# Leftover keys of an attention sweep taken in eight pieces in its middle, with constant products at the joints

## The reference

```python
scores = jnp.einsum('bhqd,bhkd->bhqk', qh, kh)       # 16 heads, 1024 queries, 6404 keys
attn = jax.nn.softmax(scores, axis=-1)
ctx = jnp.einsum('bhqk,bhkd->bhqd', attn, vh)
```

## Time and profile before

| | us |
|---|---|
| median of 3 runs | 3082.24 (3079.79 to 3084.54) |
| the profiled execution | 3080.51 |
| its span | 3078.7 |
| mean granted TensorE clock | 0.991 |

### The profile page before, as it was taken

How to read it: one execution, slowest core, us unless ns; L and a number is a source line. 1 busy time by engine, 2 the same in 40 slices (tenths; PEclk the granted TensorE clock), 3 DMA queues, 4 the chain that set the end, 5 groups by cost and what they waited for, 6 DMA issues and landing times.

```text
span 3078.7 us, 54520 instructions
## 1 busy us (share of the span) xinstructions
PE 3009.3 (98%) x18701; PEld 1140.2 (37%) x18701; DVE 467.2 (15%) x1308; ACT 2519.7 (82%) x2893; POOL 206.1 (7%) x732
## 2 busy tenths in 40 slices
PE   7999999999999899999999998999999999999999
PEld 5333333323334433333323334666522222332257
DVE  4200001001011400111101004544200000000012
ACT  3899999999933499999999995322499999999963
POOL 4000000000000000000000002000000000000000
PEclk9999999999999999999999999999999999999999
DMA  7122122112220112122211223110011111111110
GB/s 198 54 63 64 58 63 68 38 37 63 63 75 0 29 58 69 54 63 65 64 38 39 63 63 112 32 37 1 8 38 37 37 37 54 47 38 36 37 38 8
DMA packets 167028, 157.27 MB, mean 51 GB/s; under 512 B 20872, under 2 KB 121724, under 8 KB 166844
## 3 DMA queue, kind: packets, MB, share of 16 engines
q1 hardware_dynamic: 159872, 149.27, 16.1%
q0 software_dynamic: 1088, 3.34, 0.3%
q10 hardware_dynamic: 5884, 2.08, 0.3%
HBM read 121.89 MB, written 32.91 MB: 50 GB/s over the span
## 4 chain that ended last, share of the span: by engine, by line
PE 94%; DVE 3%; DMA 1%; issue 1%; ACT 1%; SPq 1%; ACTq 0%; DVEq 0%
PE PS L2343 40%; PE PS L2362 31%; PE PS L774 5%; PE PS L759 5%; PE PS L761 2%; PE PS L1114 2%; PE PS L1104 1%; PE PS L1572 1%; PE PS L1569 1%; PE PS L1148 0%; PE PS L1105 0%; PE PS L2323 0%; PE PS L2253 0%; PE PS L2329 0%; PE PS L1134 0%
## 5 line engine op out<-in xcount | busy, mean ns | idle before, releaser
L2110 ACT ACTIVATE probs<-PS 128x1024 f32<-128x1024 f32 x2496 | 2283.0, 1227 | 37.8 <-PE PS L2362 32.9
L2343 PE MATMUL PS<-probs,vr 128*32 128x512 f32 (+1 forms) x9984 | 1324.3, 603 | 1.9 <-DVE accs L2590 1.9
L2362 PE MATMUL PS<-qs,kr 35*128 35x512 f32 (+2 forms) x4992 | 1064.4, 481 | 8.7 <-ACT probs L2110 3.3
L2362 PEld LDWEIGHTS PS<-qs,kr 35*128 35x128 f32 x4992 | 448.0, 184 | 1181.9 <-ACT probs L2110 816.0
L797 ACT ACTIVATE probs<-PS 128x512 f32<-128x512 f32 x192 | 114.5, 598 | 273.6 <-PE PS L759 145.5
L1939 POOL COPY vr<-vs 128x72 f32 (+1 forms) x624 | 157.8, 253 | 2668.9 <-PE PS L2343 2466.5
L2343 PEld LDWEIGHTS PS<-probs,vr 128*32 128x32 f32 x9984 | 197.2, 108 | 339.2 <-issue 272.1
L774 PEld LDWEIGHTS PS<-wide,probs 128*128 128x128 f32 x1280 | 152.7, 195 | 17.5 <-issue 16.5
L774 PE MATMUL PS<-wide,probs 128*128 128x128 f32 x1280 | 155.1, 279 | 0.5 <-DVE kf L832 0.5
L2590 DVE COPY accs<-PS 128x512 f32<-128x512 f32 x12 | 8.3, 692 | 750.1 <-PE PS L2329 750.1
L759 PE MATMUL PS<-xT,wide 128*128 128x512 f32 x224 | 106.7, 594 | 1.0 <-DVE probs L816 1.0
(11 more groups left out here) (315 smaller groups left out, 1185.8 us busy)
## 6 DMA issues: line engine op xcount, KB each, us to landing
kr<-key_pieces SPq DMA_DIRECT2D x1248, 64.0 KB
key_pieces<-kparts SPq DMA_DIRECT2D x172, 96.0 KB, 2.8
kr<-mask_strips SPq DMA_DIRECT2D x624, 4.0 KB
values<-kf SPq DMA_DIRECT2D x34, 216.0 KB, 4.2
vs<-values SPq DMA_DIRECT2D x2, 3672.0 KB, 16.1
c_T<-turned_context SPq DMA_DIRECT2D x18, 192.0 KB, 4.0
key_pieces<-probs SPq DMA_DIRECT2D x32, 96.0 KB, 2.9
c_in<-turned_context SPq DMA_DIRECT2D x16, 192.0 KB, 4.3
```

The costliest lines, as they stand in the source:

```text
L2110: sc.activation(prob[n % RING][:, :, q0:], PS[:, bank:bank + 2, q0:], ACT.Exp, scale=SCALE).then_inc(p_ready, 1)
L2343: last = te.matmul(PS[32 * j:32 * j + 32, 7, q0:], vr[s.buf(c)][:, at_v:at_v + 32], prob[(n + j // 2) % RING][:, j % 2, q0:], start=fresh, ...
L2362: last = te.matmul(o, kr[b][own, p, :], qs[own, T8 // 2 * s.hh + p, 512 * s.qh + q0:512 * s.qh + 512], start=True, stop=True)
```

## The change

The leftover work leaves the sweep's end. The four score products are made one at a time in round 9 (LEFT_ROUND), behind quads (0,1), (1,0), (1,1) and (2,0) of that round; the exponential follows round 9 on ACT; the product of values is cut into four of 128 columns, behind the same quads of round 10. The first piece waits for what the whole did (left_in in a first sweep, bank 6 free). The item of round 9 moves to the last chunk of round 10, and that of round 10 to the first chunk of round 11. Where the rounds were one hardware loop, rounds 9 and 10 are written out between two loops. At each joint three constant products into bank 6 stand between scores(1, 0) and values(s, 0, 0), and eight into bank 5 ahead of the flag of the third attention. DVE's copy of bank 7 waits for the sweep's last values, and two other waits for pv_done make up for the order that the leftover product gave.

```diff
+LEFT_ROUND = EXP_ROUND - 1
@@ early_dve
                 dve.wait_ge(left_ready, 2)
+                dve.wait_ge(pv_done, SWEEPS[2].quads)
@@ SP, sweeps with w % 4 == 2
                                 sp.wait_ge(left_ready, s.w)
+                                sp.wait_ge(pv_done, s.quads)
@@ ACT
                             exps(c, p)
-                            if prev and (c, p) == (0, 1):
-                                exps_left(prev)
                     with act.Fori(1, EXP_ROUND) as i:
...
+                    exps_left(s)
...
-                    if s.w % NSW == NSW - 1:
-                        exps_left(s)
@@ PE, ahead of the flag of the third attention
+                idle_products(8, 5)
                 pe.wait_ge(flag_ready, a + 1)
@@ PE
-                def left_scores(s):
+                def left_free(s):
                     if s.w % NSW == 0:
                         pe.wait_ge(left_in, LEFT_IN * (a + 1))
                     if s.w:
                         pe.wait_ge(left_done, s.w)
...
+                    if s.w % NSW == 2:
+                        if a == 0:
+                            pe.wait_ge(early_ev, EARLY_AT[0] + 3)
+                        else:
+                            pe.wait_ge(r_cen, (0, 1, 3)[a])
+                    own = [(w, i) for w in range(s.w + 1) for i in range(1, ROUNDS_S) if w < s.w or i < LEFT_ROUND]
+                    pe.wait_ge(v_ev, NTILE + sum(len(later_items(w, i)) for w, i in own))
+                def left_score(s, tt):
+                    if tt == 0:
+                        left_free(s)
...
+                def left_value(s, k):
+                    if k == 0:
+                        pe.wait_ge(left_done, s.w + 1)
+                    last = te.matmul(PS[:, 7, k * P:k * P + P], v_left[:, s.hh, :], p_left[:, k * P:k * P + P], start=False, stop=True, skip_group_check=True)
...
+                def left_slot(s, i, c, g):
+                    slot = 2 * c + g - 1
+                    if i == LEFT_ROUND and 0 <= slot < 4:
+                        left_score(s, slot)
+                    if i == LEFT_ROUND + 1 and 0 <= slot < 4:
+                        left_value(s, slot)
...
                     if prev:
                         values(prev, prev.n - 1, 0)
-                        left_scores(prev)
                     scores(0, 1)
                     if prev:
                         values(prev, prev.n - 1, 1)
-                        left_values(prev)
...
+                            if prev and (c, g) == (1, 0):
+                                pe.wait_ge(v_ev, NTILE + sum(len(later_items(w, i)) for w in range(s.w) for i in range(1, ROUNDS_S)))
+                                idle_products(3, 6)
                             values(s, c - 1, g)
...
+                            if i == LEFT_ROUND:
+                                items = []
+                            if i == LEFT_ROUND + 1:
+                                items = [None] * (TC - 1) + later_items(s.w, LEFT_ROUND)
+                            if i == LEFT_ROUND + 2:
+                                items = later_items(s.w, i - 1) + items
...
                                     values(s, i * TC + c - 1, g)
+                                    left_slot(s, i, c, g)
...
-                        with pe.Fori(1, ROUNDS_S) as i:
+                        with pe.Fori(1, LEFT_ROUND) as i:
...
+                        for c in range(LEFT_ROUND * TC, (LEFT_ROUND + 2) * TC):
...
+                        with pe.Fori(LEFT_ROUND + 2, ROUNDS_S) as i:
...
                     if s.w % NSW == NSW - 1:
-                        left_scores(s)
                         for g in range(2):
                             values(s, s.n - 1, g)
-                        left_values(s)
@@ DVE
                     dve.wait_ge(left_used, s.w + 1)
+                    dve.wait_ge(pv_done, s.quads + 2 * s.n)
```

More of the change, by code:

```diff
@@ L2383, in _ @@
                                     values(s, i * TC + c - 1, g)
-                                if c < len(items):
+                                    left_slot(s, i, c, g)
+                                if c < len(items) and items[c]:
                                     later_pe(pe, *items[c])
@@ L2388, in _ @@
                     else:
-                        with pe.Fori(1, ROUNDS_S) as i:
+                        with pe.Fori(1, LEFT_ROUND) as i:
+                            for c in range(TC):
+                                for g in range(2):
+                                    scores(c, g, i)
+                                    values(s, c - 1, g, i)
+                        for c in range(LEFT_ROUND * TC, (LEFT_ROUND + 2) * TC):
+                            for g in range(2):
+                                scores(c, g)
+                                values(s, c - 1, g)
+                                left_slot(s, c // TC, c % TC, g)
+                        with pe.Fori(LEFT_ROUND + 2, ROUNDS_S) as i:
                             for c in range(TC):
```

15 lines of the change are left out of this document (7 added, 8 removed).

## The result

The changed kernel takes 3141.03 us (median; 3133.99 to 3153.87), the one before beside it on the same chip 3081.01 us (3078.21 to 3084.54). The ratio is 1.0192, interval 1.0168 to 1.0216: 60 us slower, where 22 us slower had been forecast and the range ended 33 us above the kernel before. The profiled execution after took 3144.03 us, its span is 3142.3 us, 63.6 us more than before, at a mean granted clock of 0.977 instead of 0.991.

A forecast was written before the change was run, and what follows sets the result against it. ACT's exponentials bound a sweep (1.81 us a quad, PE 0.16 us to spare). Terms: -11.9 - 5.7 + 17.2 + 1.8 + 17.0 + 3.6 + 0.4 = +22.4 us on 3080.5, 3102.9, as a median 3104.6; range 3089 to 3114.

The forecast's parts named there:

- The clock behind these waits: Behind the waits in sweeps 0, 4 and 8, PE's clock falls: 1.2 us each, +3.6 us, between 0 and 8.
- Rival C: Clock stays down longer behind the waits and meets pieces without lead: +8 to +10 us more, 3114 us; chance 0.14.
- The wait: At chunk 27 of sweeps 0, 4 and 8, PE waits for the last left load: +17.0 us, between 13 and 20.
- Rival B: Left loads land in time, so no wait: 3084 us, chance 0.05 alone; with Rival A 3071 us, chance 0.04.
- The pieces: Rounds 9 and 10, all twelve sweeps: scores 0.2, exponential 0.5, values 0.7 us, 1.4 a sweep, +17.2 us.
- The cover: PE's lead over ACT hides up to about 0.5 us of a lump of extra PE work in a sweep.
- the moved items: In six sweeps, items of rounds 9 and 10 follow the pieces without lead: 0.3 us each sweep, +1.8 us.
- Rival A: Single pieces fit PE's slack, only ACT's 0.5 us counts: +6 instead of +17.2 us, items free, 3092 us; chance 0.17.
- The joints: At nine joints between sweeps, the whole 14.1 us loss goes, less 0.25 us each for constant products: -11.9 us.
- Tails: At the ends of the three attentions, the next stage begins 1.7 to 2.0 us earlier: -5.7 us.
- Flag: Eight constants ahead of the third attention's flag delay first scores 1.0 us, win some slow stretch back: +0.4 us.
- Rival D: Constants ahead of the flag don't hold the clock: +1.0 instead of +0.4 us, inside the range; no separate chance given.

The follow-up runs named there:

- the run with the idle time filled: The changed kernel with 32 constant products (21 in sweep 8) issued ahead of the wait for the left loads; 3112.8 us, ratio 1.0105.
- pieces later: The changed kernel with its wait kept at chunk 27 of sweeps 0 and 4, first sweeps' pieces in rounds 12 and 13; 3119.9 us, ratio 1.0130.
- the spaced pieces: The changed kernel with left loads started two at a time and quads left between pieces; 3086.4 us, ratio 1.0007 to the kernel before.
- the wait alone: The kernel before with only a wait for left_in added at chunk 27 of sweeps 0 and 4; 3099.6 us, ratio 1.0059.
- the flag alone: The kernel before with only eight constant products added ahead of the flag of the third attention; 3082.8 us, ratio 1.0007.

## Why the prediction was right, and where it was wrong

The direction was right, and so was the place: the wait for the left loads outweighs what joints and tails give. The size was wrong by 38 us, and one step holds 26 of them.

*The clock behind these waits: 3.6 us forecast, 28 to 30 measured.* This is the failed step. It priced the stretch from the earlier trace rows, 0.8 to 2.9 us for a stretch of 8 to 11 us, and took for granted that the length there is the length anywhere. Behind this wait come the pieces. A quad at the low clock is 3.02 us with no piece and 3.74 with one, and in sweeps 0 and 4 the full clock isn't granted again for 44 and 31 us: until 7.7 us after the last value piece started (241.43 to 249.1), and until between the third and the fourth of them (1218.5). That all of it needs the idle time in the wait is shown, by the run with the idle time filled, which keeps the pieces. That the length comes from the pieces is likely and not shown: with pieces later it was 6.8 us twice, but in sweep 8 it was 6.8 us with them. Rival C named what happened in one sentence ("the fallen clock meets the pieces"), but its price was again three of the stretches of the earlier trace rows. The Trainium skill (TensorE: Matmul & The Clock Gate, "Why this matters for your kernels") advises against idle gaps between bursts; the three waits bear it out, at a price of 28 us.

*The wait: 17.0 us forecast, 18.6 measured.* It stands where the forecast put it, behind quad (0,1) of round 9 in sweeps 0, 4 and 8, with PE idle for 6.9, 6.8 and 4.5 us. From the start of the last load to the first piece it is 4.09 us (205.14 to 209.23), where I took 3.2 from the stores. The Trainium skill's fixed cost of about 2.0 us (DMA: Bandwidth & Descriptors, "Anatomy of one DMA") would have made the waits shorter. That section gives it for transfers that GpSimd starts, and this one is started by SP; the trace has twice as much. That the sum came so near is in part luck: for the later score pieces it took 0.3 us once a wait, not once a piece. Rival B is out: no load was in time.

*The pieces: 1.4 us a sweep and 1.8 for the moved items, 19.0 together, forecast; 24.7 measured.* The exponential (0.5 forecast, 0.47 measured) and the values (0.7 and 0.77) came as reckoned. The scores didn't: 0.2 forecast, 0.8 measured in sweeps 1, 3, 5 and 7 and about 1.3 in sweeps 9 and 11. A lone score product takes 0.42 us and not 0.30; the forecast had allowed for a change of form at the value pieces and the constants and not here. With 0.42 its own sum, 4 x 0.42 less three times the slack of 0.16 less 0.5 of cover, gives 0.7. The cover is there in the sweeps that are written out, where the first piece is free and a lump of 1.2 us loses 0.7. In sweeps 9 and 11, behind the end of a hardware loop, it isn't: the step of ACT over the first score piece is 1.33 us, so all of its 0.42 us counts, and the next two are 1.16 us, which is 0.42 less the slack. The forecast had up to 1 us for such a loop, but for fetching code.

The cover was also read from a wrong count. The window of the earlier trace rows holds 162 exponentials if those that only reach into it are counted. From the first start in it (1290.76) to the last (1439.81) are 159 steps, which need 143.7 us and take 149.0: 5.3 us are lost and not 3.5, so 0.53 us an item and 0.34 us hidden. That 0.5 us fits score pieces and lump all the same is luck. The lead isn't one number; the slack is what to plan with, as the spaced pieces show. Rival A is out: in a row, pieces don't ride along.

*The joints: -11.9 forecast, -6.9 measured.* In the first and third attention they give 8.1 us where 10.6 were forecast. It isn't the constants, which cost 0.12 us a joint on balance and not 0.25; what fails is "It all goes". Even without constants these six joints and the 24 chunks behind them give 9.0 us and not 12.1, since part of what isn't lost at the joint is lost a few chunks later. In the second attention they lose 1.2 us instead of winning. There the last products before a joint are small (exponentials of 256 columns, line 1300.41 of after), and before, the four score products of the leftovers stood in that place and the clock stayed up. Whether three constants hold it is a matter of the run: the clock fell at 11 of 21 such joints with three, at 2 of 3 with none, at none of 3 with ten, and at none of 9 in the three kernels that keep the leftover products there (before, the wait alone, the flag alone). The forecast had no term for it; it asked only what the moved work costs, not what it did for the clock where it was.

*Tails: -5.7 forecast, -5.2 measured. Flag: +0.4 forecast, 0.0 measured,* with a delay of 0.55 us instead of 1.0 (from the run with these constants alone). Rival D was right in that the clock falls in spite of the constants: later, for half as long in that run and for twice as long in the changed kernel.

What is left over are the first chunks of sweeps 0, 4 and 8, whose losses differ between these traces by up to 9 us in all, without an edit near them in some. The spread of the kernel before, 3073 to 3094 us over its runs, is larger still. That the one causes the other wasn't shown.

No version of the study beats the kernel before by more than can be measured. The best two, with early loads and spaced pieces, are level with it.

## What to carry to other kernels

Before a step is moved ahead in an engine's queue, look at when the transfers that it waits for are started, not only at how much they carry: here the last one was released by the very work that stood behind the wait, and starting the loads earlier gave back 43 of 60 us. Work that comes in small lone products is worth spreading over quads that have slack, one per two or three quads: that was 10 us better than one in each quad, which was no better than two lumps. And ask of work that leaves a thin place (a causal end, a joint) whether it was what kept the clock up there, and of a wait what the idle time in it does to the clock of what comes behind. When instructions are counted in a window to get a pace, count from start to start: those that only reach into it spoil a small difference.

## What the hardware showed that I had not expected

- The low clock can outlast its cause by far while PE is busy without a gap: 44 us behind a wait of 6.9 us, when lone products of the leftovers stood between the quads; 6.8 us behind a wait of 6.1 us when they didn't, and also 6.8 us behind a wait of 4.5 us when they did.
- It falls without any long wait as well: behind the joint 4 to 5 after, PE is busy for 7.52 of 8 us and the clock is at 0.57.
- Constants that nobody reads, 32, 32 and 21 of them put into three waits, are worth 28 us together; the wait itself hardly changes by them (7.4 us against 6.9 in sweep 0).
- A lone product of 128 rows by 512 columns between products of other forms takes 0.42 us, in a lump of four 0.30 us.
